# One kernel for two transformer blocks: the second batch normalised on VectorE, queries first in the first gather, five instruction orders written anew

## The reference

```
L0 attention: xn = layernorm(x); q, k, v = xn@Wq+bq, xn@Wk+bk, xn@Wv+bv   (16 query heads, 4 key heads, 8 channels)
              x += softmax(q k^T / sqrt(8)) v @ Wo + bo
L0 ffn:       top-2 gate of 8 from softmax(xn@Wg); x += (g1+g2) * relu(xn@w1)@w2
L1 attention: a gated state-space layer: conv of 4 taps, 16 states, a scan over the tokens, @W_out
L1 ffn:       gated ternary layers of 128 to 512 to 512 to 512 to 128
```

## Time and profile before

| | |
|---|---|
| time, median of 3 | 355.36 us |
| the profiled execution's own time | 355.43 us |
| its span, first to last instruction | 353.6 us |
| TensorE busy | 343.7 us (97%), 1754 matmuls |
| VectorE busy | 308.0 us (87%) |
| ScalarE busy | 287.8 us (81%) |
| GpSimd busy | 232.9 us (66%) |
| HBM traffic over the span | 53 GB/s |

### The profile page before, as it was taken

The page is one execution under the profiler, slowest core; times in us unless marked ns, Lnnn a source line. Parts: engine busy times, 40 slices in busy tenths (PEclk is TensorE's granted clock), DMA queues, the critical chain, the costliest instruction groups (busy, mean ns, idle before and its releaser), DMA issues.

```text
span 353.6 us, 5743 instructions
## 1 busy us (share of the span) xinstructions
PE 343.7 (97%) x1754; PEld 179.2 (51%) x1754; DVE 308.0 (87%) x530; ACT 287.8 (81%) x503; POOL 232.9 (66%) x294
## 2 busy tenths in 40 slices
PE   7999999999999999999999999999999999999996
PEld 4565634747565434434344446544455544555546
DVE  6899989989799798499999999999998978999840
ACT  3955886978688785899899969998999999689920
POOL 3553482332720201346997979999999989999990
PEclk9999999999999999999999999999999999999999
DMA  6449477936447003000000000000000000000000
GB/s 228 114 124 184 84 200 172 157 91 135 93 136 123 4 2 122 22 1 2 22 0 3 1 0 24 0 15 2 0 13 26 1 30 2 1 0 1 2 30 30
DMA packets 29198, 19.39 MB, mean 55 GB/s; under 512 B 4256, under 2 KB 28144, under 8 KB 28912
## 3 DMA queue, kind: packets, MB, share of 16 engines
q1 hardware_dynamic: 29168, 19.03, 22.4%
HBM read 13.45 MB, written 5.37 MB: 53 GB/s over the span
## 4 chain that ended last, share of the span: by engine, by line
PE 87%; DVE 6%; ACT 3%; issue 2%; POOL 1%; ACTq 0%; DVEq 0%; POOLq 0%
PE bank L1027 16%; PE bank L1016 15%; PE bank L436 7%; PE bank L423 4%; PE bank L1098 4%; PE bank L1051 4%; DVE mx L681 4%; PE bank L460 4%; PE bank L990 4%; PE bank L1071 4%; PE bank L468 4%; PE bank L1006 4%; PE bank L1007 4%; PE bank L400 3%; PE bank L1088 2%
## 5 line engine op out<-in xcount | busy, mean ns | idle before, releaser
L1367 POOL TENSOR_TENSOR acc<-acc,hb 128x512 f32<-128x512 f32 x128 | 158.3, 1267 | 16.5 <-DVE hb L1311 16.4
L1311 DVE TENSOR_TENSOR_SCAN hb<-da,bank 128x512 f32<-128x512 f32 x128 | 146.0, 1201 | 8.7 <-PE bank L990 8.1
L681 DVE TENSOR_REDUCE mx<-bank 128x2 f32<-128x512 f32 x128 | 81.6, 681 | 7.3 <-PE bank L400 4.8
L1216 ACT ACTIVATE da<-dt,nega 128x510 f32<-128x510 f32 x128 | 81.3, 709 | 0.1
L1016 PE MATMUL bank<-sil,ld 128*128 128x512 f32 x128 | 59.2, 592 | 0.0
L1027 PE MATMUL bank<-gelu,ld 128*128 128x512 f32 x128 | 58.4, 592 | 0.0
L631 ACT ACTIVATE pt<-bank 128x512 f32<-128x512 f32 x72 | 39.8, 599 | 7.0 <-PE bank L436 4.2
L423 PE MATMUL bank<-q_st,k_st 51*128 51x512 bf16 (+1 forms) x128 | 38.8, 381 | 0.5 <-ACT pt L631 0.5
L400 PE MATMUL bank<-k_st,q_st 48*128 48x256 bf16 x248 | 38.1, 272 | 0.3 <-DVE mx L681 0.2
L1027 PEld LDWEIGHTS bank<-gelu,ld 128*128 128x128 f32 x128 | 24.1, 190 | 26.0 <-issue 25.2
L1016 PEld LDWEIGHTS bank<-sil,ld 128*128 128x128 f32 x128 | 23.9, 190 | 23.2 <-issue 22.2
(11 more groups left out here) (166 smaller groups left out, 537.7 us busy)
## 6 DMA issues: line engine op xcount, KB each, us to landing
q_st<-q_scr SPq DMA_DIRECT2D x15, 192.0 KB, 3.8
q_st<-q_scr SPq DMA_DIRECT2D x7, 384.0 KB, 5.0
ld<-in_pack SPq DMA_DIRECT2D x2, 1024.0 KB, 5.6
q_scr<-qk_parts SPq DMA_DIRECT2D x8, 192.0 KB, 2.6
k_st<-k_scr SPq DMA_DIRECT2D x14, 96.0 KB, 4.7
q_scr<-qk_parts SPq DMA_DIRECT2D x8, 128.0 KB, 1.8
out<-x SPq DMA_DIRECT2D x8, 128.0 KB, 1.9
ld<-in_pack SPq DMA_DIRECT2D x1, 968.0 KB, 6.0
```

What stands on the lines that cost most here:

```text
L681: eng.tensor_reduce(mx[:, 2 * pair:2 * pair + 2, q], score_bank(b, n)[:, :].rearrange("p (h k) -> p h k", h=2), AX.X, ALU.max).then_inc(mx ...
L1216: act(da(n)[:, :, 1:T], dt[:, g % 2, c, :].rearrange("p (b n) -> p b n", b=GB)[:, :, 1:T], ACT.Exp, scale=nega[:, c, s:s + 1]).then_inc(da ...
L1311: eng.tensor_tensor_scan(hb[:, s % NPAIR, c, :], da(n).rearrange("p b n -> p (b n)"), b_bank(g, s)[:, :], 0.0, ALU.mult, ALU.add).then_inc ...
L1367: TT(acc[:, g % 2, c, :], acc[:, g % 2, c, :], hb[:, s % NPAIR, c, :], ALU.add).then_inc(add_ok, 1)
```

## The change

Five edits, by piece:

1. `inverse` no longer writes normalised rows. A new piece `subtracted` (VectorE, two instructions) does so for batch 0 and for batch 1, and ScalarE's `normalised` begins at batch 2.
2. In `fetch` the wait for `init_p` stands only ahead of the transfer of keys. For batch 0 the two transfers of queries are issued first, and the wait for the keys in HBM and the transfer of keys come last.
3. The start of VectorE's list: `clear` 0 and both first `clear_values` stand ahead of `ones`; `clear_values` 2 and 3 come before and between the first `M`.
4. GpSimd's `ones` (the memsets of `k_st`) stands behind the first gate step `G`.
5. All lists are rearranged: 9 instead of 8 `warm` at the front; in `sync` both first parts of x ahead of `head`, and the three `put` of batch 0 ahead of its three `put_keys`; in `scalar` `own_keys` 0 ahead of `k_out` 0; in `tensor` the first `S` ahead of the transposes of batch 1, and `ffn_in` 0 behind the transposes of batch 3; in `vector` `early_normalise` 1 behind the last `M`. The numbers of pieces are unchanged, but for those of edit 1.

```
-    sync="""x_in head x_in constants0 x_in ffn_weights 2*put put_keys put 2*put_keys fetch 2*put_keys 2*put put_keys
-        put fetch stack 3*put 3*rows stack fetch put_keys 2*put 2*rows put rows fetch 2*put put_keys loads stack
-        2*rows put rows put_keys loads fetch stack 2*put 2*rows put rows fetch 3*put stack 3*rows fetch stack 2*put
...
-    tensor="""8*warm xn_transposes 2*warm project project_keys warm v_gate ffn_in xn_transposes S warm 2*xn_transposes
-        S project_keys project 2*S ffn_in 3*S 2*warm xn_transposes warm 3*S ffn_out S project 3*S ffn_in 2*S
-        xn_transposes ffn_in max_rows 3*S v_gate warm 2*S ffn_out 2*S xn_transposes A S A S xn_transposes A S A S A
...
-    scalar="""deviation0 xn_out deviation0 q_out wide_out k_out normalised own_keys normalised xn_out normalised
-        2*xn_out deviation0 roots own_keys k_out q_out relu normalised gate_exp normalised relu normalised xn_out
-        q_out relu xn_out normalised negated_maxima relu gate_exp xn_out 2*E xn_out 2*E k_out 2*E q_out 3*E relu E
...
-    vector="""clear_values ones clear_values moments inverse moments wide_q inverse first_split v_out first_split
-        moments 2*M inverse M clear_values 5*M gate_sum M gate_norm M gated 6*M clear_values 2*M v_out 2*M gate_sum M
-        gate_norm 8*M gated 6*M v_out 2*M gate_sum M gate_norm M gated 10*M heads 2*M v_out M back_out 2*M residual
-        2*M gate_sum 3*M heads M gate_norm M back_out 3*M residual 3*M gated 3*M v_out M gate_sum 2*M gate_norm 2*M
...
-        back_out 3*M residual gate_sum M gate_norm M statistics gated M inverse1 2*M early_normalise M clear 3*M v_out
-        heads M back_out 2*M residual 4*M gate_sum M gate_norm gated 6*M early_normalise 5*M heads conv mul clear xm
-        clear_keys back_out mul conv zm xm residual zm mul heads mul scan conv scan conv scan 2*xm zm lift2 scan
-        back_out scan lift2 scan zm scan residual scan clear scan heads scan back_out 2*scan lift3 residual scan
...
-    gpsimd="""ones biased G biased shifted0 split_k split_q 7*G split_q maxima_split 8*G split_q maxima_split 8*G
-        split_k split_q biased maxima_split 8*G split_q maxima_split 7*G split_q G maxima_split 8*G split_q constants
...
+    sync="""2*x_in head constants0 ffn_weights x_in 3*put 3*put_keys fetch put 3*put_keys 2*put fetch stack put rows
+        put 2*rows put fetch loads stack put put_keys put 3*rows put fetch stack put_keys 3*rows 3*put put_keys loads
...
+    tensor="""9*warm xn_transposes 2*warm project warm project_keys v_gate S xn_transposes S 2*xn_transposes ffn_in
+        project_keys project 2*S ffn_in 3*S warm xn_transposes 2*warm 3*S ffn_out S project 3*S ffn_in 2*S
+        xn_transposes ffn_in max_rows 2*S warm v_gate 3*S ffn_out 2*S xn_transposes S 2*A S A xn_transposes 2*S A
+        project_keys A S A S A S project A S A S ffn_in S 2*A S max_rows A S ffn_in v_gate A S A 2*S ffn_out A S
...
+    scalar="""deviation0 xn_out deviation0 q_out wide_out own_keys k_out normalised xn_out normalised xn_out own_keys
+        xn_out deviation0 k_out q_out relu roots normalised gate_exp xn_out relu normalised q_out relu xn_out
+        normalised negated_maxima relu normalised gate_exp xn_out 2*E xn_out 2*E k_out 3*E q_out 2*E relu
+        negated_maxima 2*E relu gate_exp 4*E q_out 9*E o_out E negated_maxima 6*E gate_exp 2*E o_out 3*E q_out 2*E
...
+    vector="""clear 2*clear_values ones moments inverse subtracted moments wide_q inverse first_split v_out subtracted
+        first_split moments clear_values inverse M clear_values 7*M gate_sum M gate_norm M gated 8*M v_out 2*M
+        gate_sum M gate_norm 8*M gated 6*M v_out 2*M gate_sum M gate_norm M gated 10*M heads 2*M v_out M back_out 2*M
+        residual 3*M gate_sum 2*M heads gate_norm 2*M back_out 3*M residual 3*M gated v_out 5*M gate_sum 3*M heads 2*M
...
+        gate_norm back_out 3*M residual 3*M gated 2*M v_out 2*M gate_sum 2*M gate_norm gated 2*M v_out 5*M heads M
+        back_out 2*M gate_sum residual statistics M gate_norm 2*M gated inverse1 M early_normalise 6*M v_out heads M
+        back_out 2*M residual gate_sum 4*M gate_norm M gated 11*M heads conv mul clear_keys xm back_out mul conv zm xm
+        early_normalise zm mul residual clear heads mul scan conv scan conv xm scan xm zm lift2 scan zm scan back_out
+        scan lift2 scan residual 2*scan clear heads scan back_out scan lift3 residual scan statistics scan lift3
+        inverse1 3*scan 2*conv 2*mul 2*zm scan 2*mul 5*scan residual1 scan residual1 10*scan 2*conv scan zm 2*mul zm
...
+    gpsimd="""G ones shifted0 split_k split_q 3*G biased 4*G split_q maxima_split 7*G biased G split_q maxima_split
+        8*G split_k split_q maxima_split 7*G biased split_q G maxima_split 5*G constants G split_q 2*G maxima_split
+        9*G split_q 2*G maxima_split 9*G maxima_split 4*G maxima_split split 2*start 8*add start 6*add start 6*add
...
@@ -307,11 +308,11 @@
 
         def fetch(b):
             q_out, k_out = scratch(b)
-            reached(eng, kscr_ok, group_of(b), 16 * NRUN, 16 * NRUN)
             reached(eng, s_ps, b - 2, NH, NH)
-            if b < 2:
-                eng.wait_ge(init_p, 2 + b)
+
             def k_rows(lo, hi):
+                if b < 2:
+                    eng.wait_ge(init_p, 2 + b)
                 return eng.dma_start(k_st[b % 2][0:ROWS, lo:hi, :],
                                      k_out[lo * HD:hi * HD].rearrange("(h d) c n -> (d c) h n", d=HD))
 
@@ -319,16 +320,18 @@
                 return eng.dma_start(q_st[b % 2][0:ROWS, lo:hi, :],
                                      q_out[lo * HD:hi * HD].rearrange("(h d) c n -> (d c) h n", d=HD))
 
-            if b == 0:
-                k_rows(NOWN // G, NKV).then_inc(sc0_ok, 16)
+            if b > 0:
+                reached(eng, kscr_ok, group_of(b), 16 * NRUN, 16 * NRUN)
+                k_rows(0, NKV).then_inc(sc_ok[b % 2], 16)
+            reached(eng, scr_ok, b, 16 * NRUN, 16 * NRUN)
+            if b > 0:
+                q_rows(0, NH // 2).then_inc(sc_ok[b % 2], 16)
             else:
-                k_rows(0, NKV).then_inc(sc_ok[b % 2], 16)
-                reached(eng, scr_ok, b, 16 * NRUN, 16 * NRUN)
-                q_rows(0, NH // 2).then_inc(sc_ok[b % 2], 16)
-            if b == 0:
-                reached(eng, scr_ok, b, 16 * NRUN, 16 * NRUN)
                 q_rows(NOWN, NH // 2).then_inc(sc0_ok, 16)
             q_rows(NH // 2, NH).then_inc(sc2_ok[b % 2], 16)
+            if b == 0:
+                eng.wait_ge(kscr_ok, 16 * NRUN)
+                k_rows(NOWN // G, NKV).then_inc(sc0_ok, 16)
             if b == LAST:
                 for c in range(2):
                     eng.dma_start(q_st[1][ROWS + c * HD:ROWS + (c + 1) * HD, :, :],
@@ -552,8 +555,8 @@
 
         def normalised(b):
             eng.wait_ge(st_rs, 2 * x_part(b) + 2)
-            if b == 1:
-                eng.wait_ge(xn_ok, 1)
+            if b == 2:
+                eng.wait_ge(xn_ok, 2)
             reached(eng, xnT_ps, b - 2, 1, 1)
             for q in range(TPB):
                 c = b * TPB + q
@@ -662,15 +665,18 @@
             if k == len(X_PARTS) - 1:
                 return
             if k == 0:
-                eng.wait_ge(st_rs, 1)
-                for c in range(lo, hi):
-                    last = eng.tensor_scalar(xn[0][:, c, :], x_sb[:, c, :], mv[:, c, 0:1], rstd[:, c:c + 1],
-                                             ALU.subtract, ALU.mult)
-                last.then_inc(xn_ok, 1)
                 return
             eng.wait_ge(st_rs, 2 * k + 1)
             eng.scalar_tensor_tensor(nmr[:, lo:hi], mv[:, lo:hi, 0], -1.0, rstd[:, lo:hi],
                                      ALU.mult, ALU.mult).then_inc(st_rs, 1)
+
+        def subtracted(b):
+            eng.wait_ge(st_rs, 2 * x_part(b) + 1)
+            for q in range(TPB):
+                c = b * TPB + q
+                last = eng.tensor_scalar(xn[b % 2][:, q, :], x_sb[:, c, :], mv[:, c, 0:1], rstd[:, c:c + 1],
+                                         ALU.subtract, ALU.mult)
+            last.then_inc(xn_ok, 1)
 
         def maxima(n):
             b, n = n // NH, n % NH
@@ -766,7 +772,7 @@
```

65 lines of the change are left out of this document (31 added, 34 removed).

## The result

The changed kernel takes 358.31 us in the median of 4 runs (358.23 to 358.42), the kernel before, on the same chip, 355.32 (355.24 to 355.6, 4 runs). The ratio is 1.0080 with a 95% interval from 1.0067 to 1.0094: 3.0 us slower. The profiled execution took 358.26 us, its span is 356.5. The forecast was 356.2 with a range to 357.1: the sign was right and the size was not.

The account below looks back on a forecast made before the run. TensorE was taken as the bound (87% of the chain of waits, full from 200 us), with the start paced by one thread through three engines. 355.43 + 1.2 (start) + 0.1 (pairs) - 0.5 (last maxima) = 356.2 us, range 354.2 to 357.1.

Parts of the forecast that it names:

- Warm-up: TensorE's start: 18 warm matmuls, not 16, begun 0.52 us later; batch 0's transposes 0.8 us later (bounds 0.45 and 0.95).
- ScalarE's thread: Start: the 0.86 us removed is replaced by a wait for `subtracted` 1; `k_out` 1 at 16.1, +1.2 us with warm-up.
- GpSimd beside VectorE: Rival, chance 0.05: `k_st` memsets double the times of `subtracted` and the keys' split, 0.6 us on the thread, 356.8.
- The gather: First key gather before `S` 4: issued at 15.3, not what `S` 4 waits for; 0, upper bound +0.4 us.
- Score pieces: TensorE's neighbouring `A` and `S`: 99 pairs instead of 101, +0.43 us at most, taken as +0.1.
- The last maxima: Near 129 us: `early_normalise` 1 (1.10 us) moved behind the last five `M` that TensorE waits for; -0.5 us.
- The faster case: Rival, chance 0.25: ScalarE's 0.86 us saving arrives and the last maxima give all 1.1; 353.9, or 354.7 with half.
- The absorbed case: Rival, chance 0.25: the start's 1.2 us is swallowed, or half, where VectorE or a transfer waits anyway; 355.5.

Follow-up runs that it names:

- The late lists: The kernel before, with its own code and lists up to the third `max_rows` (52 us) and the changed kernel's lists behind: 356.51 us, ratio 1.0030.
- A mixture of the two sets of lists: The kernel before up to `max_rows` of batch 6 (114 us), the changed kernel's lists only behind that: 361.26 us, ratio 1.0153.
- both start edits undone: The changed kernel with GpSimd's `k_st` memsets ahead of the gate step again and the warm-up as before: 356.68 us, ratio 1.0028.

## Why the prediction was wrong

**Warm-up: right.** 6.25 us for the first transposes, predicted 6.35 with bounds 6.0 and 6.5. Undoing it gives back 0.6 us by the medians, both with the memsets where the change put them and with them moved. There is luck in the closeness: with the same list the transposes came at 5.77 in one trace, below the 5.9 that the prediction had named as a sign against it.

**ScalarE's thread: the walk was right in its size, its reason only in part.** The wait for VectorE's `subtracted` did take the place of the work removed, and of the 2.0 us at `S` 4, 1.2 are this walk with the warm-up in it (19.25 with the memsets moved away). But the prediction held that the 0.86 would arrive if that wait were gone, and it didn't: with `subtracted` 1 early the time is that of before (355.68 against 355.67), because the transposes of batch 1 hang on `v_out` and `ffn_in`. With `ffn_in` out of their way as well `S` 4 still came at 17.9, so TensorE's own work up to it seems to set it; no run shows that alone.

**GpSimd beside VectorE: the step that failed.** The prediction made it a rival of 0.05, priced at 0.6 us: "The rows speak against it: VectorE's two memsets at 1.43 and 1.83 take 0.38 each with GpSimd's memset (0.71 to 2.55) beside them". Those rows showed a memset beside a memset, and nothing of the TENSOR_SCALAR and the CAST that were to stand there. It measured 0.79 us at `S` 4 and 0.8 to 1.3 in time, by ratios and by medians. Its price of 0.6 wasn't far off, but by luck: a doubling in proportion was assumed, and the cost is the rest of the memset beside it, 0.78 us for the normalising and 0.69 for the CAST, beside memsets of 0.95 and 1.03. ScalarE's first normalising, at 12.58 and not 11.79 as with the memsets first, carries it on. The Trainium skill (SBUF — State Buffer, Who interferes with whom) had both halves: copy, cast and tensor_scalar with their operands in SBUF can take the pair of ports that VectorE and GpSimd share, whoever issues first has it for the whole instruction, and the other "fully blocks". The runs agree with it in what is held and what isn't: operands in a bank, bn_stats and a TENSOR_TENSOR with two SBUF inputs beside a memset (0.41 at 13.56) weren't held. Who issued first they don't always tell: the TENSOR_SCALAR that took 1.13 is shown from 11.37, 0.09 ahead of the memset that held it, while its twin before it ran to 11.45. The prediction had cited a shorter line of another page, without the ports' rule of who waits how long, and set rows above it that did not bear on it.

**The gather: right.** The keys were issued at 16.16 (predicted 15.3), 0.9 late with the held split of the keys ahead of them, and `S` 4 still came right behind TensorE's own work.

**Score pieces: the bound was too wide.** Two pairs fewer were bounded by 0.43 and taken as 0.1. One of the two measured nothing; the other wasn't tested.

**The last maxima: wrong.** -0.5 was forecast from TensorE's two waits (0.25 and 0.20), and moving the piece gave 0.0. Both waits are still there. VectorE waits for TensorE's scores in the time set free (0.46 and 0.42 us), so its last `M` ends no earlier. The prediction saw this ("But the scores themselves limit") and took -0.5 even so.

**The late lists: the second step that failed, 0.80 to 0.95 us.** Of them the prediction had priced pairs and last maxima (-0.4) and taken the rest as nothing, with doubts about dozens of places that it had not walked. So this is 1.2 to 1.35 us of the error, as large as GpSimd's part. The traces say where most of it lies, and the two stretches named next repeat to 0.02 us in every traced kernel with the same lists there. From `max_rows` of batch 3 to that of batch 4 it takes 14.82 us and not 14.38: 0.44, of which 0.21 goes with `constants` and `gm` and the other half is open. From `heads` of batch 5 to `heads` of batch 6 it takes 21.26 and not 20.67: 0.59, with the same pieces on TensorE and the same wait of 0.20. Another 0.13 lies between 100 and 117 us, and behind 152 us 0.3 is won back. The 0.59 is in TensorE's own order. One place of it is two `pv` that stood next to each other before:

```profile
131.93 1.92 PE L436 MATMUL bank<-pt,v_sb 128*32 128x512 f32 x16
```

```profile
133.60 1.06 PE L439 MATMUL bank<-pt,v_sb 128*32 128x512 f32 x8
...
135.56 1.06 PE L439 MATMUL bank<-pt,v_sb 128*32 128x512 f32 x8
```

Together they took 1.85 us (131.93 to 133.78). Apart, with `max_rows` and three `A` between them, each takes 0.99 to the next start (133.60 to 134.59, 135.56 to 136.55). An `A` with a `pv` behind it takes 0.32 us to the next start (145.54 to 145.86) where with another piece behind it it took 0.23 (143.62 to 143.85). No run puts these pieces back alone, so it is argued and not shown that they are the cause. As causes, TensorE's order in the first stretch but for one pair, the early normalising and `constants` count for 0.00, 0.00 and 0.08 us in their traces. A mixture of the two sets of lists has waits of its own (361.26), and so can't divide the loss further.

The faster case didn't come about: it hung on `subtracted` 1 ending before 10.7 us, and where that was brought about (8.5) the time stayed as before. The absorbed case failed too, since nothing of the start's 2.0 us was taken up by 69 us.

The sum as measured, in excess over the kernel before: memsets and warm-up together 1.87 (1.3 and 0.6), the late lists 0.80, the rest of the start 0.32; that is the 2.99.

## What to carry to other kernels

Before moving work of GpSimd, list what VectorE does in the same microseconds, by kind of instruction and by where its operands lie. A TENSOR_SCALAR or a CAST between SBUF operands waited here for the whole rest of GpSimd's instruction (1.13 and 0.97 us where 0.34 and 0.28 are their own), so a long memset is best done before the thread starts, or in small pieces. A row is evidence only for its own kind of instruction. And before a piece is moved out of the way of a wait, ask what its engine would do in the time set free: here it waited for the very engine that was waiting for it.

## What the runs showed of the hardware that I had not expected

Waiting for each other goes both ways: the memset at 5.41 us took 1.09 and not 0.95 with VectorE's normalising under way.

TensorE's change of pace doesn't come at the same moment in each execution, though the granted clock is shown as 1.00. With the same list and the same start at 2.43, 18 warm matmuls took 4.02 us in the changed kernel (above) and 3.50 us in the kernel with the memsets cut in four, where the transposes came at 5.77:

```profile
2.43 3.50 PE L517 MATMUL bank<-warm_in 128*128 128x256 bf16 x18 [2.43 <-DVE warm_in L644]
```

And with the start at 1.86, four warm matmuls took 0.60 at 5.80 us in the kernel before, but 1.06 in the kernel with both start edits undone, and the projections behind them 1.01 and not 0.67:

```profile
5.86 1.06 PE L520 MATMUL bank<-warm_in 128*128 128x256 bf16 x4
6.71 1.01 PE L527 MATMUL bank<-xnT,head 128*128 128x256 f32 x2
```

That is 0.5 to 0.7 us between executions whose lists are the same up to there on TensorE. The first part of x doesn't land at the same moment either: VectorE's first bn_stats, which waits for it, began between 3.25 and 3.56 us in seven traced kernels that are the same on all engines up to 52 us, the kernel before among them. Their first `max_rows` starts between 27.09 and 28.07. What a start loses stays: the latest of them, the kernel with `gate_norm` moved, is 0.83 us behind the kernel before there and 0.85 at the last group of matmuls. So times have to be compared with this in mind, and traces stretch by stretch.
